# State-space scan in a decoder kernel: the first layer norm and parts of the step inputs move between VectorE, ScalarE and GpSimd

## The reference

```python
x_dbl = jnp.einsum('bld,ed->ble', hidden_states, W_xproj)
dt_low, Bm, Cm = x_dbl[..., :64], x_dbl[..., 64:80], x_dbl[..., 80:]
delta = softplus(jnp.einsum('blr,dr->bld', dt_low, W_dt) + b_dt)
dA = jnp.exp(delta[..., None] * A)                        # A = -exp(A_log), 256 x 16
dBx = (delta * x)[..., None] * Bm[:, :, None, :]
h = dA_t * h + dBx_t                                      # along the sequence
y = jnp.einsum('bdn,bn->bd', h, C_t)
x = _layernorm(x + y)                                     # (x - m) / sqrt(v + 1e-5)
```

## Time and profile before

| | us |
|---|---|
| median of 3 runs | 1593.45 |
| lowest, highest | 1589.97, 1598.83 |
| the profiled execution: time | 1589.16 |
| its span, first to last instruction | 1587.3 |
| VectorE busy over the whole span | 1067.6 (67%) |
| TensorE, ScalarE, GpSimd busy | 1243.0, 739.4, 696.1 |
| mean granted clock of TensorE | 0.897 |

### The profile page before, as it was taken

The page is one execution under the profiler, slowest core; times in us unless marked ns, Lnnn a source line. Parts: engine busy times, 40 slices in busy tenths (PEclk is TensorE's granted clock), DMA queues, the critical chain, the costliest instruction groups (busy, mean ns, idle before and its releaser), DMA issues. The chain is left out here.

```text
span 1587.3 us, 23084 instructions
## 1 busy us (share of the span) xinstructions
PE 1243.0 (78%) x7183; PEld 878.4 (55%) x7183; DVE 1067.6 (67%) x2113; ACT 739.4 (47%) x1585; POOL 696.1 (44%) x533
## 2 busy tenths in 40 slices
PE   6777777777777749999999999931299999999950
PEld 2222322322223227777787777721289898999950
DVE  4898998989999955555565555568545555555523
ACT  4555454654546425555545555420045455555424
POOL 2465565756657553333233332222524445554430
PEclk8898998989999879999989999855699999999985
DMA  3000000000000012222222222210214434443225
GB/s 95 13 14 1 14 0 13 14 0 13 0 1 0 1 29 58 70 66 57 70 63 70 67 56 70 64 66 0 83 61 88 81 98 108 83 100 71 38 27 211
DMA packets 60731, 80.64 MB, mean 51 GB/s; under 512 B 10208, under 2 KB 52896, under 8 KB 57504
## 3 DMA queue, kind: packets, MB, share of 16 engines
q1 hardware_dynamic: 47808, 58.70, 12.8%
q0 software_dynamic: 12288, 17.05, 6.5%
q10 hardware_dynamic: 576, 4.19, 0.6%
HBM read 42.00 MB, written 21.14 MB: 40 GB/s over the span
## 5 line engine op out<-in xcount | busy, mean ns | idle before, releaser
L489 POOL TENSOR_TENSOR scan_hc<-scan_state,scan_c_sb 128x1024 f32<-128x1024 f32 x128 | 309.0, 2416 | 213.1 <-DVE scan_state L423 202.4
L423 DVE TENSOR_TENSOR_SCAN scan_state<-scan_decay,scan_drive_ps 128x512 f32<-128x512 f32 x256 | 297.3, 1203 | 0.2
L217 PE MATMUL scan_y_ps<-scan_hc,all_ident 128*128 128x512 f32 x520 | 276.4, 658 | 3.1 <-POOL scan_hc L489 3.1
L1603 DVE TENSOR_TENSOR expert_hid_lo<-expert_hid,expert_hid_hi 128x512 fp32r<-128x512 f32 x128 | 88.5, 691 | 175.5 <-ACT expert_hid_hi L1587 166.2
L1500 POOL DMA_INDIRECT acc<-expert_rows,expert_lst x64 | 111.9, 1749 | 177.2 <-DVE expert_rows L1629 162.6
L1582 ACT ACTIVATE expert_hid<-expert_h_ps,expert_b 128x512 f32<-128x512 f32 x128 | 88.2, 689 | 198.9 <-PE expert_h_ps L523 171.7
L320 ACT ACTIVATE scan_decay<-scan_delta,scan_a_neg 128x508 f32<-128x508 f32 x256 | 169.4, 716 | 7.2 <-POOL scan_delta L483 7.2
L348 ACT ACTIVATE scan_c_sb<-scan_c_ps 128x512 f32<-128x512 f32 x128 | 76.6, 598 | 200.5 <-PE scan_c_ps L210 200.5
L416 DVE TENSOR_TENSOR scan_drive_ps<-scan_dx,scan_b_ps 128x512 f32<-128x512 f32 x256 | 162.8, 681 | 7.0 <-DVEq L400 2.5
L205 PE MATMUL scan_b_ps<-scan_bcs,scan_sel 96*128 96x512 bf16 x128 | 52.9, 413 | 138.8 <-DVE scan_drive_ps L416 138.7
L217 PEld LDWEIGHTS scan_y_ps<-scan_hc,all_ident 128*128 128x128 f32 x520 | 105.8, 207 | 87.5 <-issue 78.8
(11 more groups left out here) (228 smaller groups left out, 2708.7 us busy)
## 6 DMA issues: line engine op xcount, KB each, us to landing
attn_qz<-attn_q_parts SPq DMA_DIRECT2D x128, 128.0 KB, 2.6
weights_w<-w SPq DMA_DIRECT2D x16, 1024.0 KB
table<-all_row SPq DMA_DIRECT2D x32, 132.0 KB, 1.8
scan_xT<-xT SPq DMA_DIRECT2D x8, 512.0 KB, 4.0
attn_ctxT<-ctxT SPq DMA_DIRECT2D x32, 128.0 KB, 2.5
acc<-all_row SPq DMA_DIRECT2D x32, 128.0 KB, 1.7
final_a<-acc SPq DMA_DIRECT2D x4, 1024.0 KB, 7.1
out<-final_o ACTq DMA_DIRECT2D x4, 1024.0 KB, 5.7
```

The lines of the kernel that those rows point to most:

```text
L217: last = pe.matmul(y_ps[k][:], ident[0][:], hc[:, n % RING, k, :], start=False, stop=(n == NS - 1))
L423: dve.tensor_tensor_scan(state[:, n % RING, k, :], decay[:, n % RING, k, :, :].rearrange("p b t -> p (b t)"), drive_ps[k][:], 0.0, ALU.mul ...
L489: pool.tensor_tensor(hc[:, n % RING, :, :], state[:, n % RING, :, :], c_sb[:, n % RING, :].unsqueeze(1).broadcast_to([P, KH, GT]), ALU.mul ...
L1603: dve.tensor_tensor(hid_lo[:, f % RING_H, :], hid[:, f % 2, :], hid_hi[:, f % RING_H, :].bitcast(F32), ALU.subtract).then_inc(hid_ready, 1)
```

## The change

Five edits. (1) The moments of a block are merged by one aggregate instruction for each block (4 in a row) in place of six small operations over all 4; the variance is then column 1 of `moment`. (2) The normalising of the 4 blocks is done by ScalarE, at step 7, as x times rstd plus shift; GpSimd makes shift = 0 - mean times rstd in two small operations behind its product of step 5. (3) The two casts of the split are done by ScalarE (`middle_part`, step 9), and VectorE's last subtraction (`last_part`) stands at step 10. (4) dx is multiplied by GpSimd, behind its product of step 12. (5) So that the order holds, `project`, the copies and `split` are one step later (7 and 8), `step_size` too (9), and softplus has its parts and its exponential together at step 10.

```diff
@@ -104,9 +104,10 @@
...
         stats = s.sb("stats", [P, GB, 6])
-        moment = s.sb("moment", [P, 4, GB])
-        mean = s.sb("mean", [P, GB])
-        var = s.sb("var", [P, GB])
+        moment = s.sb("moment", [P, GB, 2])
+        scaled = s.sb("scaled", [P, GB])
+        shift = s.sb("shift", [P, GB])
+        zero = s.sb("zero", [P, GB])
         ln_var = s.sb("ln_var", [P, GB])
@@ -146,7 +147,10 @@
...
         stats_ready = s.sem("stats_ready")
+        stats_seen = s.sem("stats_seen")
         mv_ready = s.sem("mv_ready")
+        scaled_ready = s.sem("scaled_ready")
+        shift_ready = s.sem("shift_ready")
         lv_ready = s.sem("lv_ready")
@@ -191,7 +195,7 @@
...
                     pe.wait_ge(bc_high, g + 1)
-                    pe.wait_ge(bc_step, 5 * g + 1)
+                    pe.wait_ge(bc_step, 4 * g + 1)
                     for k in range(KH):
@@ -249,9 +253,9 @@
...
                         if not final:
-                            if n == 6:
+                            if n == 7:
                                 project(i + par, 1 - par)
-                            if n == 8:
+                            if n == 9:
                                 step_size(i + par, 1 - par)
@@ -327,11 +331,25 @@
...
                 def inv_std(g):
-                    act.wait_ge(mv_ready, 3 * (g + 1))
+                    act.wait_ge(mv_ready, g + 1)
                     act.wait_ge(normed, g + 1)
-                    act.activation(ln_var[:], var[:], ACT.Ln, bias=eps[:, 0:1]).then_inc(lv_ready, 1)
+                    act.activation(ln_var[:], moment[:, :, 1], ACT.Ln, bias=eps[:, 0:1]).then_inc(lv_ready, 1)
                     act.wait_ge(lv_ready, g + 1)
                     act.activation(rstd[:], ln_var[:], ACT.Exp, scale=-0.5).then_inc(rstd_ready, 1)
+
+                def normalise(g):
+                    act.wait_ge(shift_ready, g + 1)
+                    for j in range(GB):
+                        last = act.activation(x1[:, ds(GB * g + j, 1), :].rearrange("p o d -> p (o d)"),
+                                              m_ps[j // 2][:, (j % 2) * D:(j % 2 + 1) * D], ACT.Identity,
+                                              bias=shift[:, j:j + 1], scale=rstd[:, j:j + 1])
+                    last.then_inc(normed, 1)
+
+                def middle_part(i, par):
+                    g = 2 * i + par
+                    act.wait_ge(bc_step, 4 * g + 1)
+                    act.activation(bcs[par][32:64, :], bc_rest[32:64, :], ACT.Copy).then_inc(bc_step, 1)
+                    act.activation(bc_mid[64:96, :], bc_rest[64:96, :], ACT.Copy).then_inc(bc_step, 1)
 
@@ -350,13 +368,16 @@
...
                             inv_std(g)
+                        if n == 7:
+                            normalise(g)
                         if not final:
-                            if n == 7:
+                            if n == 8:
                                 copy_low(g + 1)
...
                             if n == 9:
+                                middle_part(i + par, 1 - par)
+                            if n == 10:
                                 softplus_parts(g + 1)
-                            if n == 10:
                                 softplus_exp(g + 1)
@@ -366,6 +387,7 @@
...
                 high_part(0, 0, first=True)
+                middle_part(0, 0)
                 act.wait_ge(const_loaded, 16 * consts)
@@ -383,6 +405,7 @@
...
                 inv_std(GROUPS)
+                normalise(GROUPS)
 
@@ -391,19 +414,13 @@
...
                     dve.tensor_tensor(bc_rest[:], m_ps[1][0:96, :], bcs[par][:], ALU.subtract).then_inc(bc_step, 1)
-                    dve.wait_ge(bc_step, 5 * g + 1)
-                    dve.tensor_copy(bcs[par][32:64, :], bc_rest[32:64, :]).then_inc(bc_step, 1)
-                    dve.tensor_copy(bc_mid[64:96, :], bc_rest[64:96, :]).then_inc(bc_step, 1)
-                    dve.wait_ge(bc_step, 5 * g + 3)
+
+                def last_part(i, par):
+                    g = 2 * i + par
+                    dve.wait_ge(bc_step, 4 * g + 3)
                     dve.tensor_tensor(bcs[par][64:96, :], bc_rest[64:96, :], bc_mid[64:96, :], ALU.subtract).then_inc(bc_step, 1)
-                    dve.wait_ge(bc_step, 5 * g + 4)
-                    dve.sem_inc(bc_step, 1)
+                    dve.wait_ge(bc_step, 4 * g + 4)
                     dve.sem_inc(bcs_ready, 1)
-
-                def step_inputs(i, par):
-                    g = 2 * i + par
-                    dve.wait_ge(delta_ready, g + 1)
-                    dve.tensor_tensor(dx[par][:], delta[par][:].rearrange("p k b t -> p k (b t)"), xT[par][:], ALU.mult).then_inc(dx_ready, 1)
 
@@ -429,15 +446,12 @@
...
                     last.then_inc(stats_ready, 1)
-                    merge_moments(dve, stats, stats_ready, g + 1, moment, mean, var, mv_ready, g)
-
-                def normalise(g):
-                    dve.wait_ge(rstd_ready, g + 1)
+                    dve.wait_ge(stats_ready, g + 1)
+                    dve.wait_ge(shift_ready, g)
+                    dve.sem_inc(stats_seen, 1)
                     for j in range(GB):
-                        last = dve.tensor_scalar(x1[:, ds(GB * g + j, 1), :].rearrange("p o d -> p (o d)"),
-                                                 m_ps[j // 2][:, (j % 2) * D:(j % 2 + 1) * D],
-                                                 mean[:, j:j + 1], rstd[:, j:j + 1], ALU.subtract, ALU.mult)
-                    last.then_inc(normed, 1)
+                        last = dve.bn_aggr(moment[:, j, :], stats[:, j, :])
+                    last.then_inc(mv_ready, 1)
 
@@ -447,12 +461,10 @@
...
                             statistics(g)
-                        if n == 5:
-                            normalise(g)
-                        if n == 7 and not final:
+                        if n == 8 and not final:
                             split(i + par, 1 - par)
-                        if n == 13 and not final:
-                            step_inputs(i + par, 1 - par)
+                        if n == 10 and not final:
+                            last_part(i + par, 1 - par)
 
@@ -461,7 +473,7 @@
...
                 dve.tensor_scalar(a_neg[:], a_exp[:], -1.0, None, ALU.mult).then_inc(a_ready, 1)
-                step_inputs(0, 0)
+                last_part(0, 0)
                 with dve.Fori(0, GROUPS // 2 - 1) as i:
@@ -470,7 +482,6 @@
...
                 statistics(GROUPS)
-                normalise(GROUPS)
 
@@ -482,6 +493,18 @@
...
 
+                def step_inputs(i, par):
+                    g = 2 * i + par
+                    pool.wait_ge(delta_ready, g + 1)
+                    pool.tensor_tensor(dx[par][:], delta[par][:].rearrange("p k b t -> p k (b t)"), xT[par][:], ALU.mult).then_inc(dx_ready, 1)
+
+                def shifts(g):
+                    pool.wait_ge(rstd_ready, g + 1)
+                    pool.tensor_tensor(scaled[:], moment[:, :, 0], rstd[:], ALU.mult).then_inc(scaled_ready, 1)
+                    pool.wait_ge(scaled_ready, g + 1)
+                    pool.wait_ge(normed, g + 1)
+                    pool.tensor_tensor(shift[:], zero[:], scaled[:], ALU.subtract).then_inc(shift_ready, 1)
+
                 def outputs(q, n):
@@ -493,21 +516,28 @@
...
                         outputs(STEPS * g + n, n)
+                        if n == 5:
+                            shifts(g)
                         if not final:
...
                                 step_sizes(i + par, 1 - par)
+                            if n == 12:
+                                step_inputs(i + par, 1 - par)
 
...
                 pool.sem_inc(decay_ready, 2)
+                pool.memset(zero[:], 0.0)
                 pool.memset(hc[:, RING - 2:RING, :, :], 0.0).then_inc(zeroed, 1)
...
                 step_sizes(0, 0, first=True)
+                step_inputs(0, 0)
                 with pool.Fori(0, GROUPS // 2 - 1) as i:
...
                 group(GROUPS // 2 - 1, 1, final=True)
+                shifts(GROUPS)
 
```

## The result

| | before | after |
|---|---|---|
| median of 4 runs, us | 1596.14 | 1542.32 |
| lowest, highest | 1589.97, 1601.09 | 1540.5, 1546.79 |
| the profiled execution: time, span | 1589.16, 1587.3 | 1540.5, 1538.7 |
| the scan's length: first drives to VectorE's first instruction behind the last scan | 532.9 | 479.7 |

The ratio is 0.968, with a 95% interval from 0.965 to 0.971: the kernel is 3.2% faster. 1545 was predicted. The median of before is higher than in the table further up because a fourth run, of 1601.09 us, was added.

The account below looks back on a forecast made before the run. VectorE was taken to bound the scan, a third of the program. Direct savings of 36.7 us plus 11.5 us of waits made 48 us, from the median 1593.45 to 1545, range 1536 to 1560.

Parts of the forecast that it names:

- Direct sum: VectorE's scan work: 8.5 statistics, 14.3 normalising, 6.3 split, 9.2 dx, less 1.6 at the ends: 36.7 us saved.
- Statistics: Four aggregates take 0.6 us where the merge has 1.66, eight times: 8.5 us saved on VectorE.
- late pieces: Rival, chance 0.10: aggregates wait for GpSimd or ScalarE's normalising holds project; about 8 us return, giving 1553.
- a late dx: Slower case, chance 0.03: dx in GpSimd's queue holds the next group's first drives beyond 4.1 us of cover.
- The cover of the normalising: Slack between ScalarE's normalising, done at 196.2, and project's start at 196.9: 0.7 us.
- Ends: Losses outside the overlapped groups: 1.0 us for dx at the start, 0.6 us for statistics and normalising at the end.
- Waits: VectorE's waits before split and drives shrink as TensorE's clock stays higher: 8.5 + 3 = 11.5 us, between nothing and 14.6.
- `project` and `split` both move by one step, so their distance, and with it the wait, stays: Split part: moving both by one step was claimed to leave VectorE's wait before split unchanged.
- The change shortens the first to about 2.6 and takes away the second: TensorE's idle gaps: statistics gap from 3.70 to about 2.6 us, normalising gap gone, so 2.4 GHz more often at project.
- The clock rival: Chance 0.18: TensorE's clock falls just as often, waits stay at 21.4 and 4.5 us, only direct sum counts: 1557.
- The deeper gain: Chance 0.05: waits before split all fall to 1.62 us, those before drives to none: 1542, perhaps 1537 read.
- a lateness of 11 to 12 us of dx: Slower case: 11 us eats the 48 us gain, 12.1 gives 1602; said to take four more GpSimd operations.

Follow-up runs that it names:

- e8: Kernel before with only project, copies, split, step_size and softplus moved as in the change; scan 537.6 us against 532.9, ratio 1.002.
- e1: Kernel before with only the aggregate in place of the merge of moments; scan 526.0 us against 532.9, ratio 0.997.
- e2: Changed kernel with the normalising back on VectorE at step 5; scan 497.7 us against 479.7, ratio to before 0.980.
- e6: Changed kernel with four useless VectorE instructions in the old normalising's place; scan 493.2 us against 479.7, ratio to before 0.972.
- e5: Kernel before with unread filler products on TensorE in its four idle gaps per group; scan 531.9 us against 532.9, ratio 0.998.
- e4: Changed kernel with the two casts and last subtraction back on VectorE at step 8; scan 494.6 us against 479.7, ratio to before 0.977.

## Why the prediction was right

Direct sum. Statistics were predicted at 8.5 us and gave 9.8: the four aggregates take 0.38 us behind a wait of 0.17, and the next drives start before the last one ends, so 0.46 us where 0.6 was taken, and the merge had cost a little more than its 1.66. The normalising's 14.3 and dx's 9.2 came as reckoned; split gave 6.9 for 6.3. The handed-over pieces cost about what the rows said: the normalising 1.93 us on ScalarE for 2.1, each cast 0.63 for at most 0.6, dx 2.36, a small GpSimd operation 0.20. Neither late pieces nor a late dx came: no drives of step 0 wait for it. The cover of the normalising was smaller than the 0.7 us reckoned in some groups, between 0.3 and 0.9, since ScalarE begins it 1.2 to 1.8 us after the shift is there. It held.

Ends. At the start 1.0 us of loss was predicted and 1.1 of gain came; dx itself took its 2.36, but between profiles the first drives start anywhere from 23.8 to 27.5 us. At the end the loss was 1.8 for 0.6. The statistics, shift and normalising that were moved lost 0.3 of it (5.35 us from the last statistics to attention, before 5.04); 1.5 are TensorE's last sum, which took 3.50 us, mostly at 1.2 GHz, where it took 1.98 before (the rows are in the last section). Nothing in the sum had that term.

Waits. 11.5 us were predicted and 12.4 came (10.1 and 2.3), all seven waits at 1.62, where the estimate had allowed for some to stay. For the scan alone 49.6 was predicted (48 and the 1.6 of the ends) and 53.2 measured; that the whole span came out closer, 48.6 for 48, is luck, since the untouched phases took 3.9 us more in this profile. By the medians the gain is 53.8 us, with a before that is itself 2.7 us above the 1593.45 that the forecast started from. The window over the scan was forecast at about 485 us and above 95% busy; from the first drives to 0.8 us behind the last scan, as in the earlier trace rows, it is 480.6 us long, and VectorE is busy for 96%.

The total was right, but one step under the waits was not: "`project` and `split` both move by one step, so their distance, and with it the wait, stays". Moving them does change the wait, by 8.3 of the 10.1 us (e8), since one step later TensorE has caught up. And "The change shortens the first to about 2.6 and takes away the second" was named as the cause. The first gap did become shorter (2.45 us instead of 3.70 in the third group), but shortening it alone gives 1.7 us (e1), and bringing the second back returns 2.7 to 3.5 (e2, e6). So the later step is enough for most of it, and so is a clock kept up at the old step (e5), but the shorter first gap is not. That TensorE's clock lengthens the waits is shown by e5, which takes them all to 1.62 with VectorE's work and the steps as they were; that the gaps of VectorE's extras lower it, by e4 and e6. The clock rival (waits stay) is refuted for this kernel. The deeper gain, at 0.05, was nearly what happened; the waits before drives kept 2.2 us.

Two slips in the working changed nothing. VectorE's first slice is at 4, not at 8 or 9. And a lateness of 11 to 12 us of dx would take five more GpSimd operations of 2.36 us, not four.

What stays open is why a gap of the same length lowers TensorE's clock at one time and not at another. Behind `split` a gap of 2.9 to 3.0 us lowered it in three of seven groups before, five in e4, six in e1 and seven in e8. The 4 us more of waits before drives in e1 and e8 go with this count; whether the edits raise it or one execution has it so by chance, no run tells.

The edits don't add up one by one. From the whole they cost 18.0, 14.9 and 9.7 us to take back; put on the kernel before, the aggregate is worth 6.9 and the steps -4.7, both with the waits that the clock brought in that execution. The sum worked because it was made for the change as a whole.

## What to carry to other kernels

Where one engine is the bound and another feeds it in small products, take a job off the first by its length, and then look at what the second does in the gap: when its clock falls there, place the next large product a step later or fill the gap, and look at the row of the wait again. When a job is moved by a step, follow what its results start on the other engines (here delta, GpSimd's queue and dx), and let a short instruction with two SBUF operands start while GpSimd is between operations, or near the end of one. Put a broadcast that the bound engine waits for ahead of half of a large product, not behind all of it.
